# Normalising attention after the value product, with TensorE forming the sums, the value bias folded into the output bias, and layer norm 2 as one GpSimd pass

## What is computed

```python
x = layer_norm(hidden_states, ln1_w, ln1_b)
q = (x @ q_w + q_b)          # split into 16 heads, likewise k and v
k = (encoder_hidden_states @ k_w + k_b)
v = (encoder_hidden_states @ v_w + v_b)
scores = jnp.einsum('bhqd,bhkd->bhqk', q, k) * scale
scores = jnp.where(mask, scores, mask_value)
attn = jax.nn.softmax(scores, axis=-1)
out = jnp.einsum('bhqk,bhkd->bhqd', attn, v)     # heads joined again
out = out @ cproj_w + cproj_b
hidden = out + residual
y = layer_norm(hidden, ln2_w, ln2_b)
y = jax.nn.gelu(y @ fc_w + fc_b, approximate=True)
return hidden + y @ proj_w + proj_b
```

## Time and profile before

| what | value |
|---|---|
| median of 3 runs | 170.68 us (170.66 to 171.85) |
| the profiled execution | 171.03 us |
| its span in the trace | 169.2 us |
| mean granted TensorE clock | 0.968 of full speed |
| busy: PE, DVE, ACT, POOL | 146.0, 101.1, 98.6, 87.0 us |
| mean of one DVE split: `ff_hi`, `ff_lo` (128x512) | 457, 692 ns |
| mean of one POOL pass over 128x256 (L389) | 734 ns |
| matmuls of an fc unit, of a pj unit, start to start in the timeline | 0.24, 0.12 us |
| chain that ended last | PE 57%, POOL 17%, DVE 9%, issue 7%, DMA 4%, ACT 3% |

### The profile page before, as it was taken

How to read it: one execution, slowest core, us unless ns; L and a number is a source line. 1 busy time by engine, 2 the same in 40 slices (tenths; PEclk the granted TensorE clock), 3 DMA queues, 4 the chain that set the end, 5 groups by cost and what they waited for, 6 DMA issues and landing times.

```text
span 169.2 us, 3520 instructions
## 1 busy us (share of the span) xinstructions
PE 146.0 (86%) x1260; PEld 111.3 (66%) x1260; DVE 101.1 (60%) x243; ACT 98.6 (58%) x242; POOL 87.0 (51%) x146
## 2 busy tenths in 40 slices
PE   7599999999986888197998665957999999999993
PEld 6365678788754264074675544645787999888993
DVE  2435525897975343990589797795678521488221
ACT  2017977789769755735778667966967333344000
POOL 8935617468888952572431976799361634000000
PEclk9969999999999999759999999999999999999999
DMA  1995320202101200000000000000000010000001
GB/s 50 344 326 175 66 62 0 66 0 62 43 25 62 62 0 0 0 6 0 0 4 6 0 4 0 4 0 0 4 0 0 4 61 32 31 0 6 31 31 62
DMA packets 6786, 6.89 MB, mean 41 GB/s; under 512 B 1044, under 2 KB 6194, under 8 KB 6770
## 3 DMA queue, kind: packets, MB, share of 16 engines
q1 hardware_dynamic: 5808, 5.85, 11.1%
q10 hardware_dynamic: 674, 0.56, 1.0%
q0 software_dynamic: 288, 0.27, 0.9%
HBM read 5.62 MB, written 1.05 MB: 39 GB/s over the span
## 4 chain that ended last, share of the span: by engine, by line
PE 57%; POOL 17%; DVE 9%; issue 7%; DMA 4%; ACT 3%; ACTq 1%; POOLq 0%
PE psum L784 53%; DMA ys<-in_ctx_dram 4%; POOL probs L381 4%; POOL us L344 3%; POOL rstd L308 2%; PE psum L1019 2%; POOL wfc_lo L320 2%; POOL wpj_lo L320 1%; DVE smax L738 1%; POOL hidT_lo L372 1%; POOL rows L325 1%; POOL rows L389 1%; DVE psums L625 1%; DVE probs L749 1%; DVE xn L641 1%
## 5 line engine op out<-in xcount | busy, mean ns | idle before, releaser
L381 POOL TENSOR_TENSOR probs<-probs,pinv 128x512 f32<-128x512 f32 x16 | 16.5, 1055 | 9.7 <-DVE pinv L630 9.7
L344 POOL TENSOR_SCALAR us<-uext,rinv 128x128 f32<-128x128 f32 x32 | 12.4, 399 | 13.9 <-DVE rinv L604 13.3
L784 PE MATMUL psum<-wpj_hi,ff_hi 128*128 128x256 f32 x64 | 18.3, 287 | 0.0
L784 PE MATMUL psum<-wpj_hi,ff_lo 128*128 128x256 f32 x64 | 18.1, 283 | 0.0
L784 PE MATMUL psum<-wpj_lo,ff_hi 128*128 128x256 f32 x64 | 18.1, 283 | 0.0
L398 ACT ACTIVATE ys<-psum,vec 128x512 f32<-128x512 f32 x16 | 10.9, 687 | 9.3 <-PE psum L784 9.2
L683 DVE TENSOR_REDUCE nmax<-psum 128x2 f32<-128x512 f32 x16 | 10.3, 685 | 9.9 <-PE psum L784 9.9
L784 PE MATMUL psum<-att,us 128*128 128x256 f32 x64 | 15.2, 381 | 0.7 <-POOL us L344 0.7
L625 DVE TENSOR_REDUCE psums<-probs 128x8 f32<-128x512 f32 x16 | 10.6, 660 | 8.5 <-ACT probs L540 8.3
L443 ACT ACTIVATE att<-psum,nmax 128x256 f32<-128x256 f32 x32 | 14.7, 471 | 0.3 <-DVE nmax L683 0.2
L784 PE MATMUL psum<-hidT_hi,wfc_hi 128*128 128x512 f32 x32 | 13.2, 414 | 1.1 <-POOL hidT_lo L372 1.1
(11 more groups left out here) (115 smaller groups left out, 367.6 us busy)
## 6 DMA issues: line engine op xcount, KB each, us to landing
wstage<-in_L_xattn_fc_w_dram SPq DMA_DIRECT2D x4, 256.0 KB, 5.2
wstage<-in_L_xattn_proj_w_dram SPq DMA_DIRECT2D x4, 256.0 KB, 2.7
out_dram<-rows SPq DMA_DIRECT2D x8, 128.0 KB, 1.7
ys<-in_ctx_dram SPq DMA_DIRECT2D x1, 512.0 KB, 6.3
rows<-in_x_dram SPq DMA_DIRECT2D x1, 512.0 KB, 7.4
ys<-in_ctx_dram ACTq DMA_DIRECT2D x1, 384.0 KB, 7.0
rows<-in_x_dram SPq DMA_DIRECT2D x1, 384.0 KB, 5.8
wk<-in_L_xattn_k_w_dram SPq DMA_DIRECT2D x1, 256.0 KB, 6.7
```

The source lines that it names most:

```text
L344: pool.tensor_scalar(us[:, n % 2, e, j, :], uext[:, n % 2, j, e * C:e * C + P], rinv[:, n % 2, e, j:j + 1], 1.0, ALU.mult, ALU.mult).then_ ...
L381: pool.tensor_tensor(half, half, pinv[:, n % 2, k].unsqueeze(2).broadcast_to([P, H // 2, C]), ALU.mult).then_inc(S["probs_ready"], 1)
L784: return pe.matmul(dst, lhsT, rhs, start=start, stop=stop)
```

## The change

In the attention, the exponentials are no longer multiplied by their inverse sums. DVE's `sum_of_probs` and `inverse_of_sum` and POOL's L381 go. Instead PE forms the sums with four more matmuls behind the heads of each pair, from the turned exponentials and a constant matrix `block_ones`, in the layout of the heads. ACT takes Ln of the sums and then Exp with scale -1, and DVE multiplies the heads by that while moving them out of psum (`heads_normed`), which replaces ACT's two `hdT` passes. The value bias passes through the normalised attention unchanged, so v_b @ cproj_w is computed once, in `wtx(0)`, and added to `cproj_b` by DVE in `relu_in(0)`. Layer norm 2 becomes one subtract and multiply on POOL in place of `shift` on POOL and `hn` on ACT. PE's transposes of the probabilities now wait for the exponentials themselves.

```diff
@@ gpsimd, hidden_norm(n)
-                pool.tensor_scalar(shift[:, n % 2, :], mv[:, n % 2, 0:1], rstd[:, n % 2, :], -1.0, ALU.mult,
-                                   ALU.mult).then_inc(S["hid_shift"], 1)
+                wait(pool, "hid_turned", n - 1)
+                pool.tensor_scalar(hn[:, n % 2, :], rows[:, n, :], mv[:, n % 2, 0:1], rstd[:, n % 2, :], ALU.subtract,
+                                   ALU.mult).then_inc(S["hid_normed"], 1)
@@ gpsimd, step
-                n = t - AT + 1
-                if 0 <= n < N:
-                    for i, k in enumerate(HEAD_HALVES):
-                        wait(pool, "probs_inv", 2 * n + i + 1)
-                        half = probs[:, n % 2, i * BANK:(i + 1) * BANK].rearrange("p (h k) -> p h k", k=C)
-                        pool.tensor_tensor(half, half, pinv[:, n % 2, k].unsqueeze(2).broadcast_to([P, H // 2, C]),
-                                           ALU.mult).then_inc(S["probs_ready"], 1)
@@ scalar, step: n = t - AT - 1
                     wait(act, "heads_made", n + 1)
-                    for g in range(G):
-                        identity(hdT[:, g, :], psum[:, HEADS, g * P:(g + 1) * P], col(V_B + g), 1.0, "heads_ready")
+                    if n == 0:
+                        wait(act, "mix_normed", 2 * N)
+                    wait(act, "heads_ready", n)
+                    act.activation(sums_ln[:], halfbank(HEADS, 1), ACT.Ln).then_inc(S["sums_ln"], 1)
+                    wait(act, "sums_ln", n + 1)
+                    act.activation(sums_inv[:], sums_ln[:], ACT.Exp, scale=-1.0).then_inc(S["sums_inv"], 1)
@@ scalar, step: n = t - AT - 2
-                    act.activation(hn[:, n % 2, :], rows[:, n, :], ACT.Identity, bias=shift[:, n % 2, :],
-                                   scale=rstd[:, n % 2, :]).then_inc(S["hid_normed"], 1)
@@ vector, relu_in(0)
+                    dve.wait_ge(vb_made, 1)
+                    dve.wait_ge(w_loaded["cb"], 16)
+                    dve.tensor_tensor(cproj_b[:], halfbank(WTX, 1), cproj_b[:], ALU.add).then_inc(attn_b_ready, 1)
@@ vector
-            def sum_of_probs(n, i): ...
-            def inverse_of_sum(n, i): ...
+            def heads_normed(n):
+                wait(dve, "sums_inv", n + 1)
+                wait(dve, "attn_made", n)
+                dve.tensor_tensor(hdT[:].rearrange("p g t -> p (g t)"), halfbank(HEADS, 0), sums_inv[:],
+                                  ALU.mult).then_inc(S["heads_ready"], 1)
@@ vector, step (behind the two subtractions of pair a + 1)
-                if 0 <= n < N:
-                    sum_of_probs(n, 0)
+                if 0 <= t - AT - 1 < N:
+                    heads_normed(t - AT - 1)
                 if 0 <= t - AT - 2 < N:
                     hidden_mean_var(t - AT - 2)
-                if 0 <= n < N:
-                    inverse_of_sum(n, 0)
-                    sum_of_probs(n, 1)
-                    inverse_of_sum(n, 1)
@@ tensor, wtx(0)
+                    pe.wait_ge(w_loaded["c"], 16)
+                    pe.wait_ge(vb_cols_ready, G)
+                    for c in range(G):
+                        ins = mm(halfbank(WTX, 1), vb_cols[:, c, :], wc[:, c, :], c == 0, c == G - 1)
+                    ins.then_inc(vb_made, 1)
@@ tensor, step, behind the heads
+                    for j in range(J):
+                        ins = mm(psum[32 * j:32 * (j + 1), HEADS, D:2 * D], block_ones[:].rearrange("p b d -> p (b d)"),
+                                 prT[:, j * G:(j + 1) * G, :].rearrange("p g t -> p (g t)"))
                     ins.then_inc(S["heads_made"], 1)
@@ tensor, step
-                        wait(pe, "probs_ready", 2 * n + i // (HP // 2) + 1)
+                        wait(pe, "probs_exp", 2 * n + i // (HP // 2) + 1)
@@ tensor, step
-                    wait(pe, "heads_ready", 2 * (n + 1))
+                    wait(pe, "heads_ready", n + 1)
```

More of the change, by code:

```diff
@@ L86, in xattn_two_layers @@
         cproj_b = sb("cproj_b", [P, D])
+        block_ones = sb("block_ones", [P, 2, HD])
         proj_b = sb("proj_b", [P, D])
@@ L114, in xattn_two_layers @@
         rstd = sb("rstd", [P, 2, 1])
-        shift = sb("shift", [P, 2, 1])
         xn = sb("xn", [P, 2, D])
@@ L120, in xattn_two_layers @@
         smax = sb("smax", [P, H])
-        psums = sb("psums", [P, 2, H])
-        pinv = sb("pinv", [P, 2, H])
+        sums_ln, sums_inv = csln, csinv
         prT = sb("prT", [P, HP, P])
@@ L125, in xattn_two_layers @@
         hn = sb("hn", [P, 2, D])
+        vb_cols = hn[:, 0, :].rearrange("p (g t) -> p g t", g=G)
         hidf = sb("hidf", [P, G, P])
@@ L329, in x1_plus_bias @@
                 if n == 0:
-                    pool.wait_ge(w_loaded["cb"], 16)
+                    pool.wait_ge(attn_b_ready, 1)
                     pool.wait_ge(w_loaded["pb"], 16)
@@ L549, in _ @@
                     queries_bias(1, 1)
-                n = t - AT - 2
-                if 0 <= n < N:
-                    wait(act, "hid_shift", n + 1)
-                    wait(act, "hid_turned", n - 1)
-                    act.activation(hn[:, n % 2, :], rows[:, n, :], ACT.Identity, bias=shift[:, n % 2, :],
-                                   scale=rstd[:, n % 2, :]).then_inc(S["hid_normed"], 1)
                 mlp_units(t + 0.6)
@@ L565, in _ @@
             ins.then_inc(diag_zeroed, 1)
+            for b in range(2):
+                for d in range(2):
+                    dve.memset(block_ones[b * C:(b + 1) * C, d, :], float(b == d)).then_inc(block_ready, 1)
             dve.wait_ge(ident_ready, 1)
@@ L618, in relu_in @@
                 wait(dve, "relu_out", n - 1)
+                if n == 0:
+                    dve.wait_ge(vb_made, 1)
+                    dve.wait_ge(w_loaded["cb"], 16)
+                    dve.tensor_tensor(cproj_b[:], halfbank(WTX, 1), cproj_b[:], ALU.add).then_inc(attn_b_ready, 1)
                 dve.tensor_tensor(rin[:, n % 2, :], halfbank(WTX, 0), mixn[:],
                                   ALU.subtract).then_inc(S["relu_in"], 1)
-            def sum_of_probs(n, i):
-                wait(dve, "probs_exp", 2 * n + i + 1)
-                half = probs[:, n % 2, i * BANK:(i + 1) * BANK].rearrange("p (h k) -> p h k", k=C)
-                dve.tensor_reduce(psums[:, n % 2, HEAD_HALVES[i]], half, AX.X, ALU.add).then_inc(S["probs_sum"], 1)
-            def inverse_of_sum(n, i):
-                wait(dve, "probs_sum", 2 * n + i + 1)
-                wait(dve, "probs_ready", 2 * (n - 1))
-                dve.reciprocal(pinv[:, n % 2, HEAD_HALVES[i]],
-                               psums[:, n % 2, HEAD_HALVES[i]]).then_inc(S["probs_inv"], 1)
+            def heads_normed(n):
[3 more added lines that the diff above has]
+                                  ALU.mult).then_inc(S["heads_ready"], 1)
             def high_part(c):
@@ L719, in _ @@
                                           ALU.mult).then_inc(keys_b_ready, 1)
+                    for g in range(G):
+                        dve.tensor_scalar(vb_cols[:, g, :], ones[:], col(V_B + g), None,
+                                          ALU.mult).then_inc(vb_cols_ready, 1)
                 if 0 <= t < N and t in SPLIT:
@@ L997, in _ @@
                                          vals[:, n, e, g * J + j, :], prT[:, j * G + g, e * C:(e + 1) * C])
+                    if n == 0:
+                        pe.wait_ge(block_ready, 4)
+                    for j in range(J):
+                        ins = mm(psum[32 * j:32 * (j + 1), HEADS, D:2 * D], block_ones[:].rearrange("p b d -> p (b d)"),
+                                 prT[:, j * G:(j + 1) * G, :].rearrange("p g t -> p (g t)"))
                     ins.then_inc(S["heads_made"], 1)
```

11 lines of the change are left out of this document (4 added, 7 removed).

## The result

| | before | after |
|---|---|---|
| median of 5 runs each, us | 170.68 | 172.78 (172.62 to 175.18) |
| ratio after to before | | 1.0133, 95% interval 1.0077 to 1.0188 |
| repeated in a later set of runs | | 1.0126, interval 1.0077 to 1.0174 |
| from the scores of pair 2 to the first fc unit | 33.42 | 32.25 |
| from the first fc unit to the last write of the rows | 50.51 | 53.42 |

The changed kernel is 1.3% slower, 2.1 us. That is inside the range, and 2.6 us less than the 4.7 that I forecast.

What follows compares the result with a forecast made beforehand. The prediction took PE to bound the first layer and MLP, and waits on DVE's sums with ACT's queue the attention step. 0.87 + 3.84 = 4.7 us on the median 170.68 gave 175.4 us, range 172.5 to 178.5.

Steps and rivals of the forecast that it cites:

- First layer, +0.87: First layer, PE without gaps: two fp32 matmuls for v_b @ cproj_w add 0.87 us, lower bound 0.
- Attention, +0.15: Attention: the first fc unit of the MLP starts at 116.30 instead of 116.15 us, 0.15 later.
- late start: Attention's start: `heads_normed` queues behind DVE's subtractions, so the scores of pair 3 start at 89.65 instead of 87.91 us.
- Loop D: Attention loop over DVE and PE: mask, maximum, subtractions, `heads_normed`, cproj product, next mask; claimed 5.1 us a step.
- Loop A: Attention loop over ACT and PE: copies, heads, sums, Ln, Exp, `hidf`, `hidT_hi`, exponentials, copies; claimed 5.47 us a step.
- S: PE's time for the new sums of one pair in the attention: taken as 0.55 us, bounds 0.45 and 1.8.
- MLP, +3.69: MLP: 1.10 us for two sets of sums on PE, 0.3 + 1.0 + 1.3 of waits for ACT with six more loads.
- POOL's new pass: Layer norm 2's pass over 128x256 on POOL: some 0.73 us, covered up to twice that price.
- the loads hide: Rival, MLP: table loads run during ACT's waits and PE's 2.6 us of waits do not form; 172.8 us, chance 0.12.
- POOL's pass was the bound: Rival, attention: POOL's pass over the probabilities set the step, so the kernel gets faster; 168.7 us, chance 0.05.
- The sums did not run one after another: Denies a rival, attention: sums run in a row at 1.8 us, a step takes 6.7 us; 183 us, chance 0.08.
- that rival's 184 us: Rival, ACT: a table switch costs another 1.28 us beside each load, 8.8 us for seven; 184 us, chance 0.03.

Runs made afterwards that it cites:

- layer norm 2 alone: Kernel before the change, with only layer norm 2 changed to one subtract-and-multiply pass on POOL: 173.55 us, ratio 1.0119 to the kernel before.
- both with `hn` on ACT: Layer norm 2 restored in the changed kernel (175.74 us), and in the changed kernel with reciprocal for pairs 6 and 7 and `heads_normed` between DVE's subtractions (171.73 us).
- the fastest: Changed kernel with a DVE reciprocal replacing Ln and Exp for pairs 6 and 7, and `heads_normed` between DVE's two subtractions: 170.9 us, ratio 0.9977 to before.

## Why the prediction was only half right

- **First layer, +0.87**: right to the hundredth, and nothing behind it absorbed it.
- **Attention, +0.15: this step failed.** It came out at -1.17, and the first fc unit started 1.1 us earlier than before (115.05 for 116.15) with the 0.87 of the first layer already in it, where I had it 1 us later. The sentence that fell is "Three shorter steps just pay for the late start". The late start formed (the scores of pair 3 after 6.74 us, forecast 6.92), and so did both loops. Loop D measured 5.01 for 5.1. Loop A measured 5.18 for 5.47, three times over, and that is 0.87 of the 1.32. Its parts: S is 0.44, the lower end of my bounds, and not 0.55, so four column groups run at once and not three; the copies' end to the start of the heads is 0.05 for 0.13 (109.84 + 1.05 to 110.94); and ACT's passes are some 0.10 closer together.

  For S I had read the heads as holding PE some 0.6 us, which is the distance from their start to that of the `hn` transposes (105.70 to 106.29 in the kernel before). In the changed kernel the sums start 0.48 us behind them (110.94 to 111.42), so 0.1 of it went with the step to another kind of matmul, and 1.8 us of passes in 0.48 are nearly four at once. The ends that I added are often no ends for the next pass: Exp is listed to 107.33 + 0.42 = 107.75, and `hidf` starts at 107.66. The rest of the 1.32 is small pieces: 0.18 at the late start, 0.07 in loop D, 0.09 from the scores of pair 4 to the heads of pair 2, and 0.12 from the heads of pair 5 to the first fc unit (4.11 for 4.23). I carried errors of 0.1 us in one direction through a loop that runs three times, and gave the sum a range by S alone (116.30, or 115.9 to 117.1); 32.25 us behind 82.73 is 114.98.
- **MLP, +3.69 (of the 3.84): right in mechanism, too large.** It measured +2.91. Sums: 0.88 for 1.10, the same error in S. Waits before the first pj unit: 17.77 - 15.63 - 0.88 = 1.26 us for 1.3. But they sat elsewhere: the heads of pair 7 waited about 1 us and not 0.3, behind a link that I had missed (`hidden` queued behind the splits of late Gelus), and so the cproj product of pair 7 had hardly a wait. The last piece of pj: from its first unit to the last write 35.65 us, against 34.45 in the kernels of the same pace without loads, so 1.20 for 1.3. Last, these 34.45 us are 34.88 in the kernel before, where the matmuls of the last pj units are 0.120 instead of 0.117 us apart. That is -0.43 us, a term that the prediction did not have. It goes with the kernel and not with the execution: the last four pj units and the write behind them take 11.71 to 11.72 us in the kernel before and in the three experiments that still hold the tile `shift` in memory (layer norm 2 alone, where nothing uses it, and both with `hn` on ACT), and 11.40 us in all ten traces without it. `shift` is 8 bytes in each partition and is allocated ahead of the tiles of the MLP's inputs. That the place of those tiles is the cause would fit, but no run moved them alone.
- **What no step had: -0.80** (start -0.20, clock stretch -0.60). Both differ between executions of one kernel by about as much or more. They explain part of a difference of two profiles; what of them is in the medians is open, since the changed kernel's executions had the higher clock on average. The medians moved by 2.1 us, the traces by 1.81.
- **POOL's new pass**, priced at 0.73, took 1.23 us. It was covered but for 0.25 us before 112.28, where my addition (0.9 us of cover behind a pass of 0.73) would have left 0.4 to spare.

Of the rivals, *the loads hide* gives 172.8, which the median happens to meet, and is wrong: without loads the kernel is 1.5% faster. It had left out 2.5 us of waits that were there, and not known of 1.3 us of gain in the attention, 0.4 of PE's pace and 0.2 of cheaper sums. That the median meets it is luck. *POOL's pass was the bound* falls with the steps of 5.0 to 5.2 us, which ACT and DVE set; what POOL's pass over the probabilities was worth in the kernel before was not measured, since no run takes it out alone. The sums did not run one after another, and nothing stood on ACT beside a load (seven times 1.28 us are 9.0 and not 8.8, which leaves that rival's 184 us as it is).

What stays open besides: the kernel without the product for the value bias and with the reciprocal did not run; by the terms it would be 0.87 us below the fastest.

## What to carry to other kernels

Sum the loop that a change leaves behind from the shortest believable pieces as well as from the likeliest, and multiply the difference by the number of turns: here 0.29 us in a step were 0.87 us of the result, nearly as much as the longest wait of PE. Before a function of another table is put where Gelu already runs, count its loads: two passes of 0.4 us cost 3 x 1.28 us with them, and one DVE reciprocal of 1.75 us did the same work at 2 us less in total. And behind a late pass look at everything that is queued on the other engines for its result: the longest wait of PE came from a write that needed nothing of ACT, and stood behind one that did.

## What the runs showed of the hardware

- Eight fp32 passes of 256 columns, 32 columns of the array wide and going round four groups, add 0.44 us to PE; by the earlier trace rows one such pass on the full array takes 0.22 us. So the four groups run fully side by side.
- GpSimd's subtract and multiply with two per-partition operands over 128x256 takes 1.22 to 1.23 us in the attention, its pass over two tensors of that size (`hidT_lo`) 0.73.
- Some passes of GpSimd and DVE are longer where both engines are at work: in the MLP of the changed kernel `hn` took 1.34 us at 127.74, and DVE's `ff_lo` 0.93 and 1.11 us at 128.02 and 129.40, where the others there take 0.69, as all eight did in the kernel before. With the reciprocal on DVE for pairs 6 and 7 one `hn` took 1.63. None of it was on the chain here.
- DVE's reciprocal of 128x256 out of psum takes 1.75 us, its multiplication of the same size 0.42.
- 256-column matmuls of the pj units follow each other at 0.120 us in the four kernels that hold an 8-byte tile more and at 0.117 in the ten traces of the others, 0.43 us in all.
- A table load takes 1.28 us whether the set before was that of Gelu, Ln or Exp, and the next ACTIVATE starts 0.01 to 0.02 us behind it.
